# Layer 3's expert results written plainly to rows of their own and added up at the end, the tile loop written out

## The reference

```python
def _routing(x2d, gate_w):
    logits = x2d @ gate_w.T
    rw = jax.nn.softmax(logits.astype(jnp.float32), axis=-1)
    scores = jax.nn.sigmoid(logits.astype(jnp.float32))
    _, sel = jax.lax.top_k(scores, TOP_K)                    # TOP_K = 4
    w = jnp.take_along_axis(rw, sel, axis=-1)
    w = w / w.sum(axis=-1, keepdims=True)
    return (w.astype(x2d.dtype), sel)

def _moe(x2d, Wg, Wu, Wd, cw):
    g = jnp.einsum('th,ehi->eti', x2d, Wg)
    u = jnp.einsum('th,ehi->eti', x2d, Wu)
    a = jax.nn.silu(g) * u * cw.T[:, :, None]
    return jnp.einsum('eti,eih->th', a, Wd)
```

## Time and profile before

| | before |
|---|---|
| median of 3 runs | 1300.6 us (1300.33 to 1304.45) |
| the profiled execution | 1301.26 us, its span 1299.5 us |
| busy PE, DVE, POOL, ACT | 1081.3, 863.2, 713.6, 666.3 us |
| routing of layer 3, first one-hot matrix to first gather | 1061 to 1077 us |
| expert tiles of layer 3 | 1077 to 1286.5 us |
| readback, additions, store | 1286.5 to 1299.5 us |

### The profile page before, as it was taken

How to read it: one execution, slowest core, us unless ns; L and a number is a source line. 1 busy time by engine, 2 the same in 40 slices (tenths; PEclk the granted TensorE clock), 3 DMA queues, 4 the chain that set the end, 5 groups by cost and what they waited for, 6 DMA issues and landing times.

```text
span 1299.5 us, 18166 instructions
## 1 busy us (share of the span) xinstructions
PE 1081.3 (83%) x5382; PEld 839.8 (65%) x5383; DVE 863.2 (66%) x1521; ACT 666.3 (51%) x1702; POOL 713.6 (55%) x480
## 2 busy tenths in 40 slices
PE   6486587778748888999999999799999737999992
PEld 3465576667515665888888888665555536887781
DVE  3886999888778975666666566769987772322221
ACT  4475355445472215777787777467652134333330
POOL 1107888888723223445444554439975205888873
PEclk8887899899868988999999999889989758999996
DMA  6594899896540004011101110304543993555566
GB/s 186 163 169 131 215 279 291 231 259 147 76 126 0 1 3 123 29 55 51 54 18 54 56 45 1 102 6 146 150 137 84 275 224 67 84 83 82 81 79 133
DMA packets 141110, 146.06 MB, mean 112 GB/s; under 512 B 34181, under 2 KB 127357, under 8 KB 141029
## 3 DMA queue, kind: packets, MB, share of 16 engines
q1 hardware_dynamic: 115556, 110.71, 29.3%
q0 software_dynamic: 24384, 33.31, 15.9%
q10 hardware_dynamic: 1088, 1.05, 0.3%
HBM read 119.04 MB, written 25.99 MB: 112 GB/s over the span
## 4 chain that ended last, share of the span: by engine, by line
PE 46%; POOL 16%; DVE 13%; issue 13%; DMA 6%; ACT 4%; another core or an unknown queue 0%; SPq 0%; ACTq 0%; POOLq 0%; DVEq 0%
PE bank L1629 4%; PE bank L1725 4%; PE bank L1692 4%; PE bank L1714 4%; PE bank L2497 3%; POOL f_sums L1050 3%; PE bank L2159 3%; DMA f_sums<-arena,put 3%; POOL arena L1036 3%; POOL y L2407 2%; PE bank L1618 2%; PE bank L1647 2%; PE bank L1703 2%; POOL arena L586 2%; DMA e_sums<-ctxT,put 2%
## 5 line engine op out<-in xcount | busy, mean ns | idle before, releaser
L566 DVE TENSOR_TENSOR_SCAN arena<-arena 128x1024 f32<-128x1024 f32 x64 | 154.3, 2411 | 14.4 <-issue 10.7
L1050 POOL DMA_INDIRECT f_sums<-arena,put x64 | 126.1, 1971 | 27.1 <-issue 15.6
L586 POOL TENSOR_TENSOR arena<-arena 128x1024 f32<-128x1024 f32 x32 | 82.4, 2575 | 94.4 <-DVE arena L566 94.4
L1036 POOL DMA_INDIRECT arena<-y_rows,slots x64 | 84.8, 1324 | 65.4 <-DVEq L1253 46.2
L2398 POOL DMA_INDIRECT e_sums<-ctxT,put x63 | 100.0, 1587 | 25.4 <-issue 16.2
L2497 PE MATMUL bank<-arena,ssm_y 128*128 x504 | 109.9, 362 | 3.2 <-ACT ssm_y L2566 1.4
L544 ACT ACTIVATE arena<-arena,ssm_A 128x255 f32<-128x255 f32 x256 | 107.9, 499 | 2.0 <-DVE arena L488 1.8
L2159 PE MATMUL bank<-yT,arena 128*128 128x512 f32 (+1 forms) x224 | 105.5, 616 | 2.2 <-ACT arena L2090 2.2
L596 PE MATMUL bank<-arena,ident 128*128 128x256 f32 x256 | 69.5, 419 | 36.3 <-DVE arena L586 32.8
L2679 DVE TENSOR_SCALAR ctxT<-bank,slot_w 128x256 f32<-128x256 f32 x63 | 30.5, 484 | 97.1 <-DMA e_sums<-ctxT,put 79.0
L555 DVE TENSOR_TENSOR arena<-arena 128x1024 f32<-128x1024 f32 x64 | 93.8, 1466 | 0.8 <-DMA arena<-bc_rows 0.7
(11 more groups left out here) (343 smaller groups left out, 2778.7 us busy)
## 6 DMA issues: line engine op xcount, KB each, us to landing
arena<-bc_rows SPq DMA_DIRECT2D x64, 512.0 KB
arena<-in_L_ffn_w_gate_dram SPq DMA_DIRECT2D x16, 256.0 KB
arena<-in_L_ffn_w_up_dram SPq DMA_DIRECT2D x16, 256.0 KB
arena<-in_L_ffn_w_down_dram SPq DMA_DIRECT2D x16, 256.0 KB
x<-in_L_ffn_w_gate_dram SPq DMA_DIRECT2D x16, 256.0 KB
y<-in_L_ffn_w_up_dram SPq DMA_DIRECT2D x16, 256.0 KB
yT<-in_L_ffn_w_down_dram SPq DMA_DIRECT2D x16, 256.0 KB
arena<-in_L_ffn_Wd_dram SPq DMA_DIRECT2D x1, 3072.0 KB, 18.0
```

The source lines that it names most:

```text
L566: nc.vector.tensor_tensor_scan(ssm_h[:, j % 2, :], ssm_decay[:, j % 2, :], ssm_in, 0.0, ALU.mult, ALU.add).then_inc(s_ssm_h, 1)
L586: ops.tensor_tensor(ssm_hC_buf[:, j % 2, :], ssm_h[:, j % 2, :], ssm_C[:, g % 2, :], ALU.mult).then_inc(s_ssm_hC, 1)
L1036: nc.gpsimd.indirect_dma_start(out=f0_xg[:, n % RING, e, :], out_offset=None, in_=y_rows, in_offset=bass.IndirectOffsetOnAxis(ap=slots[:, ...
L1050: nc.gpsimd.indirect_dma_start(out=f0_sums[m % SUMS], out_offset=bass.IndirectOffsetOnAxis(ap=put[:, m:m + 1], axis=0), in_=f0_ye[:, n % R ...
```

## The change

- The scatter writes plainly. Its target is one tensor e_rows with a row of its own for each pair: row 4 token + k, k the pair's place among the token's four, and a row behind these for each unused row of a tile. No two scatters meet, so the wait on the scatter two before goes, and so do the e_sums, their zeroing (three DMAs fewer at the start; CLEARS is 5) and the copy of x into e_sums[0].
- Routing carries 4 token + k + 1 in place of token + 1. Two index tables are made by POOL at the start (e_tok, e_none). The product with e_ot moves from ScalarE (L2553) to DVE, between the two one-hot matrices. put is computed first and slots from it by a shift.
- The readback loads e_rows by token tile, four rows of a token beside each other, eight DMAs of 512 KB into e_more, each with a semaphore of its own. DVE adds four to two, two to one, and that to x, for each of eight tiles. The output is stored by token tile, eight DMAs of 128 KB.
- e_steps writes out all the steps; the hardware loop is gone.

```diff
@@ declarations
-        e_sums = [nc.dram_tensor(f"e_sums{e}", [T + CAP, D], F32, kind="Internal").ap() for e in range(2)]
+        e_rows = nc.dram_tensor("e_rows", [4 * T + E0 * CAP, D], F32, kind="Internal").ap()
-        CLEARS = 8
+        CLEARS = 5
@@ f0_const_pool
+            nc.gpsimd.iota(e_tok[:, :, :], [[P * K3, NT], [1, K3]], base=1, channel_multiplier=K3,
+                           allow_small_or_imprecise_dtypes=True)
+            nc.gpsimd.iota(e_none[:, :], [[P, TILES]], base=K3 * T + 1, channel_multiplier=1, allow_small_or_imprecise_dtypes=True)
@@ f0_sp
-            for rows in f0_sums[1:] + e_sums[1:]:
+            for rows in f0_sums[1:]:
                 sp.dma_start(rows[0:T, :].rearrange("(i p) d -> p i d", p=P), f0_zero).then_inc(s_f0_clear, 16)
-            for rows in f0_sums + e_sums:
+            for rows in f0_sums:
                 sp.dma_start(rows[T:T + CAP, :], f0_zero[:, 0, :]).then_inc(s_f0_clear, 16)
@@ e_sp
-            sp.wait_ge(s_z_x, 2 * B)
-            sp.dma_start(e_sums[0][0:T, :].rearrange("(i p) d -> p i d", p=P), x[:, :, :]).then_inc(s_e_init[0], 16)
...
-            for b in range(B):
-                tiles = slice(TPB * b, TPB * (b + 1))
-                for dst, rows in ((x, e_sums[0]), (e_more, e_sums[1])):
-                    sp.dma_start(dst[:, tiles, :], rows[0:T, :].rearrange("(i p) d -> p i d", p=P)[:, tiles, :]
-                                 ).then_inc(s_e_more[b][0], 16)
+            for i in range(NT):
+                sp.dma_start(e_more[:, i, :, :], e_rows[i * P * K3:(i + 1) * P * K3, :].rearrange("(p k) d -> p k d", k=K3)
+                             ).then_inc(s_e_back[i][0], 16)
@@ e_pool, scatter
-                if t >= 2:
-                    wait(pool, s_e_st[(t - 2) % 4], 16 * ((t - 2) // 4 + 1))
-                if t == 0:
-                    wait(pool, s_e_init, 16)
                 nc.gpsimd.indirect_dma_start(
-                    out=e_sums[t % 2], out_offset=bass.IndirectOffsetOnAxis(ap=put[:, t:t + 1], axis=0),
-                    in_=e_ye[:, t % 4, :], in_offset=None, oob_is_err=True, compute_op=ALU.add).then_inc(s_e_st[t % 4][0], 16)
+                    out=e_rows, out_offset=bass.IndirectOffsetOnAxis(ap=put[:, t:t + 1], axis=0),
+                    in_=e_ye[:, t % 4, :], in_offset=None, oob_is_err=True).then_inc(s_e_st[t % 4][0], 16)
@@ e_steps
-            for k in range(XR):
-                step(k, k, 0)
-            with eng.Fori(1, TILES // XR - 1) as i:
-                for k in range(XR):
-                    step(i * XR + k, k, i)
-            for t in range(TILES - XR, RUN + 2):
+            for t in range(RUN + 2):
                 step(t, t % XR, t // XR)
@@ e_act
-                nc.scalar.activation(e_rhs[:, i % 2, :, 0:TILES], e_ot[:, i % 2, :, :], ACT.Copy, scale=token_1[:, i:i + 1])
@@ e_dve
+                wait(dve, s_e_ot, i + 1)
+                V.tensor_tensor(e_rhs[:, i % 2, :, 0:TILES], e_ot[:, i % 2, :, :],
+                                e_tok[:, i, :].unsqueeze(2).to_broadcast([P, K3, TILES]), ALU.mult)
...
-            dve_link(V.tensor_scalar(slots[:, :], bank[5][:, 0:TILES], 1.0, 0.0, ALU.subtract, ALU.max))
+            dve_link(V.tensor_scalar(put[:, :], bank[5][:, 0:TILES], 1.0, 0.0, ALU.subtract, ALU.max))
+            dve_link(V.tensor_scalar(slots[:, :], put[:, :], K3.bit_length() - 1, None, ALU.logical_shift_right))
             dve.sem_inc(s_e_slots[0], 1)
-            dve_link(V.tensor_scalar(slot_none[:, :], bank[5][:, 0:TILES], 0.0, none_row[:, 0:1], ALU.is_equal, ALU.mult))
+            dve_link(V.scalar_tensor_tensor(out=slot_none[:, :], in0=bank[5][:, 0:TILES], scalar=0.0, in1=e_none[:, :],
+                                            op0=ALU.is_equal, op1=ALU.mult))
...
-            for b in range(B):
-                wait(dve, s_e_more[b], 32)
-                rows = x[:, TPB * b:TPB * (b + 1), :].rearrange("p a n -> p (a n)")
-                more = e_more[:, TPB * b:TPB * (b + 1), :].rearrange("p a n -> p (a n)")
-                V.tensor_tensor(rows, rows, more, ALU.add).then_inc(s_e_x[0], 1)
+            for i in range(NT):
+                wait(dve, s_e_back[i], 16)
+                four = e_more[:, i, :, :]
+                dve_link(V.tensor_tensor(four[:, 0:2, :], four[:, 0:2, :], four[:, 2:4, :], ALU.add))
+                dve_link(V.tensor_tensor(four[:, 0, :], four[:, 0, :], four[:, 1, :], ALU.add))
+                V.tensor_tensor(x[:, i, :], x[:, i, :], four[:, 0, :], ALU.add).then_inc(s_e_x[0], 1)
@@ store_sp
-            for b in range(B):
-                wait(sp, s_e_x, b + 1)
-                sp.dma_start(rows[:, TPB * b:TPB * (b + 1), :], x[:, TPB * b:TPB * (b + 1), :]).then_inc(s_out, 16)
-            sp.wait_ge(s_out, 16 * B)
+            for i in range(NT):
+                wait(sp, s_e_x, i + 1)
+                sp.dma_start(rows[:, i, :], x[:, i, :]).then_inc(s_out, 16)
+            sp.wait_ge(s_out, 16 * NT)
```

More of the change, by code:

```diff
@@ L2298, in flamingo_kernel @@
         assert at <= ARENA
-        e_more = area(0, NT, D)
+        e_more = area(0, NT, K3, D)
         XR = 8
@@ L2337, in flamingo_kernel @@
         s_e_yrows, s_e_slots = (s_f0_yrows, 16), (s_f0_slots, 2)
-        s_e_init = (s_f0_init, 16)
         s_e_ot, s_e_rhs, s_e_oc, s_e_place = (s_f0_eq, NT), (s_f0_rhs, NT), (s_f0_oc, NT), (s_f0_place, NT)
@@ L2350, in flamingo_kernel @@
         s_e_ld = (s_x_w[0], 16 * H // 2)
-        s_e_more = [(s, 16 * SUMS) for s in s_f0_more]
+        s_e_back = [(s, 16 * SUMS) for s in s_f0_more] + [(s, 16 * B * GB) for s in s_ssm_B + s_ssm_C]
         s_e_x = (s_f0_x, B)
+        e_tok = sb("e_tok", [P, NT, K3])
+        e_none = sb("e_none", [P, TILES])
         EL = 14
@@ L2448, in e_route_pe, with e_steps @@
                 last.then_inc(s_e_place[0], 1)
-        def e_steps(eng, step):
-            for k in range(XR):
-                step(k, k, 0)
-            with eng.Fori(1, TILES // XR - 1) as i:
-                for k in range(XR):
-                    step(i * XR + k, k, i)
-            for t in range(TILES - XR, RUN + 2):
+        def e_steps(step):
+            for t in range(RUN + 2):
                 step(t, t % XR, t // XR)
@@ L2538, in step @@
                     down(t - 2, (k - 2) % 4, k - 2)
-            e_steps(pe, step)
+            e_steps(step)
         def e_act(act):
@@ L2588, in step @@
                     hT_copy(t - 1, (k - 1) % 4)
-            e_steps(act, step)
+            e_steps(step)
         def e_dve(dve):
@@ L2685, in step @@
                     evict(t - 2, (k - 2) % 4, turns * (XR // 4) + (k - 2) // 4)
-            e_steps(dve, step)
-            for b in range(B):
-                wait(dve, s_e_more[b], 32)
-                rows = x[:, TPB * b:TPB * (b + 1), :].rearrange("p a n -> p (a n)")
-                more = e_more[:, TPB * b:TPB * (b + 1), :].rearrange("p a n -> p (a n)")
-                V.tensor_tensor(rows, rows, more, ALU.add).then_inc(s_e_x[0], 1)
+            e_steps(step)
+            for i in range(NT):
[4 more added lines that the diff above has]
+                V.tensor_tensor(x[:, i, :], x[:, i, :], four[:, 0, :], ALU.add).then_inc(s_e_x[0], 1)
         s_out = sem("s_out")
```

## The result

The changed kernel took 1306.0 us, median of 8 runs (1302.3 to 1315.2), beside 1300.4 for the kernel before on the same chip (8 runs, 1297.0 to 1304.5). The ratio is 1.0061, 95% interval 1.0035 to 1.0087: slower by 5.7 us by the medians and 8 by the ratio, where 10 us less were forecast. The profiled execution took 1311.0 us with a span of 1309.2, 9.7 more than the span before.

What follows compares the result with a forecast made beforehand. GpSimd's 3.19 us a tile was taken to bound layer 3 over TensorE's 2.82. Last landing 1269.25 - 0.45 routing + 1.0 loop + 19.8 tail = 1289.6 span; plus 1.76, less 0.66 to the median: 1291 us, range 1285 to 1297.

Steps and rivals of the forecast that it cites:

- last scatter to its landing: End of layer 3's tiles: the last plain scatter lands 3.3 us after its start (bounds 2.9 and 3.85).
- The price of a plain scatter: Layer 3's scatter on GpSimd: without accumulating it costs 0.98 us like a gather, not 1.59.
- rival (a): Layer 3's scatter still costs GpSimd 1.59 us; with the longer tail the time is 1303, slower; 8%.
- The pace of the tiles: Layer 3's expert tiles: GpSimd falls to 2.56 us a tile, so TensorE's 2.82 sets the pace to the end.
- The written-out loop: Layer 3's tile steps as straight code: between nothing and two stops of 1.9 us, taken as +1.0.
- (b): Stops pile up in layer 3's written-out code, three or four of 1.9 us on the path: 1297; 9%.
- (c): The early stops in layer 3's first tiles vanish as code moves, none elsewhere: 3.9 us less, 1286; 6%.
- The routing: Before the first gather: a product moved from ScalarE to DVE nets -0.45 us.
- The tail: Readback, additions and stores after the last landing: 19.8 us (bounds 18.7 and 22), DMA and DVE ending nearly together.
- The parts at nothing: Start of the kernel: dropped clears and x store, two added iotas cost nothing, at most 0.5 us.
- The range: Whole kernel: 1285 to 1297 us, taking in (c) and most of (b), leaving out rival (a).

Runs made afterwards that it cites:

- the filler: Changed kernel with a memset of 128x96 (about 0.2 us) behind each scatter: 0.9919 of before on chip 15, 1.0041 on chip 0.

## Why the prediction was wrong

By the parts of the sum, on the profiled execution (span 1309.2 against 1289.6, 19.6 more):

| part | forecast | measured | difference |
|---|---|---|---|
| first gather starts | 1076.7 | 1075.9 | -0.8 |
| first gather to last scatter's start, loop's 1.0 with it | 189.8 | 212.8 | +22.9 |
| last scatter to its landing | 3.3 | 2.4 | -0.9 |
| landing to the end of the span | 19.8 | 18.1 | -1.7 |

**The price of a plain scatter**: right, 0.988 us for 0.98, and rival (a) is out.

**The pace of the tiles**: this is the step that failed, "TensorE sets the pace to the end". It was to be 2.82 us a tile, and it measured 3.26, which with the stop at tile 1 makes the 22.9 us of the table. On chip 2 the step is right: 187.9 us from first gather to last scatter where 189.8 were forecast, 2.82 us a tile, 0.9894 of before where the forecast was 0.9926. (The time itself, 1280.7, lies under the range even so; the kernel before is 6 us faster on that chip.) On the chip of the result, TensorE has the same work, but its signals are held. The step asked what each engine owes a tile, and that TensorE's signals might come late behind rows of GpSimd's DMAs was in no row that I had taken for such. Why they come late, and only on some chips, stays open.

**The written-out loop and rivals (b) and (c)**: wrong in mechanism. The row was there: 1.74 + 2.19 us of "another core or an unknown queue". I read it as a price of straight code, since the first tiles were straight code, and gave it 1.0 us. But the same place is also the end of the one row of DMAs 1.25 us apart that the kernel before has the earlier trace rows, and the runs point to that: in the changed kernel with the row thinned the stop goes, with the loop put back it stays (4.5 us at tile 1), and writing the loop out alone gives 0.9992. Its price was misread too: from the first gather to tile 4's silu the kernel before needs 20.8 us, against 20.1 in the traces without a hold, so the 3.93 us on the chain were worth 0.7. Rival (c), priced at 3.9, could have given back no more than that. Rival (b) had the right picture, stops amid the tiles on the path, with the wrong cause, and so too few of them: it counted three or four, there were some 18, and it let them come from the loop and not from what the change does to GpSimd's DMAs.

**The routing** (-0.45): right in sign and too small. The first gather's start varies by several us from trace to trace (1068.9 to 1079.9 over all kernels), but from the first one-hot matrix to the first gather it is 16.05 us in both traces of the old routing and 14.8 to 15.0 in all 18 of the new one: 1.0 to 1.3 us won.

**The tail**: right in mechanism, slightly too dear, 18.1 for 19.8. The additions are 1.52 apart and not 1.65, because a group begins 0.07 before the last addition of the one before has ended (1296.34 against 1295.99 + 0.42) and the links cost less than the 0.04 each that I gave them; eight times 0.13 makes 1.0 of the 1.7. DVE waits for a load once, for the first (6.7 us), and never again, so DMA doesn't bind. The landing took 2.4 us, not the 3.3 that the accumulating ones suggested.

**The parts at nothing**: no row of after contradicts them.

**The range** (1285 to 1297) took its lower and upper ends from (c) and (b), so it shared their mistake.

## What to carry to other kernels

When a change shortens the distance between GpSimd's indirect DMAs, look in the trace of before for a place where they already come that close, here the first gathers, and see what stands behind it before pricing it as something else. An idle row put down to an "unknown queue" is a cause that is still to be found, and its neighbours in time on all engines are the candidates, not only the property of the code that one has in mind. And a gain of 1% should be seen on more than one chip, with the kernel that it is measured against beside it: on chip 15 the filler looked like a cure for stops that weren't there. Count the records too: where a trace holds a third of the updates that it should, what it shows may have to do with the recording.

On chip 2 none of the versions tried was clearly faster than the changed kernel as it is (1280.7 us, 0.989), and the gather that waits for gate_up is the only one that was clearly faster than before on a chip with stops (1293.8 us, 0.9956); it wasn't run on one without.

## What the runs showed of the hardware

- TensorE's completion signals can come late together while its matmuls are recorded as running on: 1.4 to 2.6 us late in the hold printed above, up to 3.2 in the changed kernel's trace. In the traces of layer 3's tiles this happened only near rows of GpSimd's indirect DMAs 1.25 to 1.5 us apart, and DMA completions kept coming meanwhile (11 updates between 1168.80 and 1172.32).
- It depends on the chip. Chips 0, 4 and 7, and the one of the result by its times and its trace, have it; chips 2 and 15 don't, with the same kernels. The traces of the former also lack many semaphore updates (the table above), those of the latter next to none. The kernel before takes 1298.7 to 1300.4 us on the former and 1294.2 to 1294.6 on the latter. Its first hold, worth 0.7 us, doesn't explain that; the first gather's start, a median of 1076.6 us in the 12 traces of the former and 1071.3 in the 8 of the latter, could, though single traces scatter from 1068.9 to 1079.9. What sets the chips apart stays open. The packets of 4 KB of the first gathers take about the same time on both kinds (medians of 0.21 to 0.24 us in the 12 traces, 0.20 to 0.23 in the 8).
- What the held signals wait for stays open. That most holds end a fixed time after the start of GpSimd's last DMA (2.2 us after the sixth, 2.0 after the fourth in the kernel whose gather waits for gate_up) fits that GpSimd's pause lets them go, but GpSimd pauses because it waits for those signals itself, so the order of cause isn't shown. The Trainium skill (DMA: Bandwidth & Descriptors, "Latency and other measured facts") says, as its best guess at why two of the DMA engines are slower, that the descriptor rings of GpSimd's DMAs lie in the first 32 partitions of SBUF and make the ports there busier. Whether TensorE's reads or acknowledgements meet that traffic no run here shows.
- A plain indirect scatter of 128 rows of 1 KB costs GpSimd 0.988 us, against 1.587 for the accumulating one, the same when that one writes to rows of its own (1.587 in the run that accumulates into e_rows).
